# Attention kernel on one Trainium2 core: the values' low half, one context block and four rope products move between engines, and the roots move by a step

## The chip, the cores and the metric

The kernel runs on one core of a Trainium2 chip. The metric is the device time of one execution in microseconds (us), taken over several runs of the same program.

## The reference

A residual stream x of 4 sequences of 2048 rows by 256 channels goes through four layers, each of the form x = x + f(layernorm(x)): a layer that adds one row's projection to every row, a feed-forward layer, a banded attention layer and the feed-forward layer again. The attention layer is the one the change touches:

```python
q = _apply_rope(proj(Wq, bq)); k = _apply_rope(proj(Wk, bk)); v = proj(Wv, bv)
# 16 heads of 64, blocks of W = 128 rows; a block's queries see their own and the preceding block's keys, in a band
scores = jnp.einsum('bhnqd,bhnkd->bhnqk', qb, kcat) * scale
scores = jnp.where(valid[None, None], scores, -1e30)
attn = jax.nn.softmax(scores, axis=-1)
ctx = jnp.einsum('bhnqk,bhnkd->bhnqd', attn, vcat)
return merged @ Wo.T + bo
```

Rope multiplies each head's vector by cosines, and its swapped halves by sines. Every row block of a sequence has 256 keys, except the first of a sequence, which has 128.

## The kernel before, in words

The attention stage (attention_stage, from L867) works in 64 steps. A step t is one superblock S = t // 4 of four row blocks (512 rows) and one group g = t % 4 of four heads. Superblocks 0, 4, 8 and 12 begin a sequence: in their 16 steps block 0 is "alone", with 128 keys. Within a step the blocks b = 0..3 are numbered n = 4t + b.

Precision comes from splitting: a float32 value is written as a float16 high half and a float16 low half (value minus high half), and TensorE adds three products of halves. So the probabilities (prob) are split into halves, the contexts into c_halves, the values into v_h and v_l, the layer norm's rows into x_halves.

Each engine has its own fixed order, written out in a function at_step(t), and the engines meet only in semaphores. In one step:

- **TensorE** (L1739) projects queries, keys and values into two PSUM banks that these three share in turn (pr_ps, one bank per half), makes the scores of two blocks at a time (scores, L1709), multiplies turned probabilities by values (values_product, L1673, into the single bank c_ps), and makes a row block of the output (output, L1694). Values are made in values (L1623); then values_rest (L1641) adds minus the identity times v_h into the same bank, so that the bank holds value minus high half.
- **VectorE** (L1408) masks and scales the scores and takes their tops (tops, L1292, four instructions for a block), makes the probabilities' low half (p_low_of, L1308), scales the contexts (context, L1317: a reciprocal and a product), multiplies the second half of keys and queries by cosine and by sine straight from PSUM (key_product L1367, query_product L1377; two instructions each), and does the residual, layer norm moments and, once in four steps, shift_of.
- **ScalarE** (L1574) makes the exponentials, the probabilities' high half (p_high_of), v_h (v_high_of, L1477) and v_l (v_low_of, L1487), the contexts' high half (context_high), normalizes rows (normalize, x_high_of) and copies the first half of keys and queries out of PSUM (key_copy, query_copy).
- **GpSimd** (L1268) makes the rope products of the first halves from those copies (key_product, query_product), joins all products to keys and queries (key L1187, query L1198), makes the low halves of contexts (context_low) and rows (x_low_of), adds a bias (bias_rows), and once in four steps takes the roots of the layer norm (inverse_std, L1207). Twice in a step it waits for a low half of the probabilities of the same step before it goes on, and at its start for the last one of the step before (after_p_low, L1224).
- **SyncE** issues the transposing DMAs that turn probabilities, contexts and rows, and most loads.

GpSimd's order is the one that has to be followed in the prediction:

```python
after_p_low(t - 1, 3); x_low_of(t + 7)
if g == 0 and S > -2: inverse_std(S + 2)
context_low(t - 2); key_product(t + 1, 0); key_product(t + 1, 3)
after_p_low(t, 0); key(t + 1, 1); query_product(t + 1, 0)
after_p_low(t, 1); query_product(t + 1, 3); key(t + 1, 0)
query(t + 1, 1); query(t + 1, 0); bias_rows(t - 4)
```

x_low_of(t + 7) needs what ScalarE's normalize and x_high_of made a step earlier; scores(t + 1, 0) on TensorE needs both halves of keys and queries that end with query(t + 1, 0).

## Time and profile before

| what | value |
|---|---|
| median of 3 runs (range) | 1607.46 us (1604.61 to 1608.63) |
| the profiled execution's own time | 1604.13 us |
| its span, first to last instruction | 1602.3 us |
| mean granted TensorE clock | 0.985 |
| busy share of the span: TensorE, VectorE, ScalarE, GpSimd | 93%, 88%, 83%, 71% |
| a step in the middle of the attention stage | 17.9 to 19.7 us |

The profile page adds up each engine's busy time and lists the costliest groups of instructions. The trace also answers for a window of time: its timeline view prints every instruction with its start (us from the span's start) and its duration, and in brackets the idle time of the engine before it with what ended it. Neighbouring alike instructions are merged there, with their count at the end of the row. An instruction's duration includes a wait for a resource it finds taken. Starts of successive VectorE and ScalarE instructions lie some 0.08 to 0.10 us closer than their durations say, since they overlap.

### The profile page before, as it was taken

The page shows a single profiled execution, that of the slowest core. Times are in us where ns is not written, and L with a number is a line of the kernel's source. Part 1 is how long each engine was busy: PE and PEld are TensorE (multiplying, and loading weights), DVE is VectorE, ACT ScalarE, POOL GpSimd, SP SyncE. Part 2 cuts the span into 40 slices and gives each one's busy share as a digit, 9 for nine tenths or more (in the row PEclk, how much of TensorE's full clock was granted, in tenths as well). Part 3 has the DMA queues.
Part 4 walks back from the last instruction along what each step waited for, and adds up shares of the span by engine and source line. Part 5 has one row for each costly group of instructions (what it writes and reads, how often), then busy time and mean ns, then how long its engine had stood idle before and what let it go on. Part 6 is the DMA issues. An engine that isn't in the chain of part 4 may idle for free. (4 is left out here: it accounts for less than half of the span.)

```text
span 1602.3 us, 46976 instructions
## 1 busy us (share of the span) xinstructions
PE 1492.1 (93%) x16866; PEld 1142.8 (71%) x16866; DVE 1402.0 (88%) x3859; ACT 1324.3 (83%) x2442; POOL 1141.7 (71%) x911
## 2 busy tenths in 40 slices
PE   5999978899999999999999999999999999779998
PEld 4888745577777677766767777767776777668887
DVE  5999668999999999999999999999998999857885
ACT  5999768888888888888888888888888888749996
POOL 4665367778787887878787878787888777623443
PEclk8999989999999999999999999999999999979999
DMA  5232338899999999999999999999999998962331
GB/s 213 93 123 92 103 68 141 163 175 175 182 176 173 172 171 172 176 180 177 171 174 169 169 183 178 173 178 176 168 166 172 173 164 163 173 148 83 107 108 67
DMA packets 729886, 247.94 MB, mean 155 GB/s; under 512 B 689588, under 2 KB 716472, under 8 KB 729656
## 3 DMA queue, kind: packets, MB, share of 16 engines
q1 hardware_dynamic: 711816, 228.93, 75.8%
q10 hardware_dynamic: 17840, 16.00, 3.7%
q8 instruction: 137, 2.24, 0.6%
q14 instruction: 93, 0.76, 0.2%
HBM read 47.73 MB, written 25.17 MB: 45 GB/s over the span
## 5 line engine op out<-in xcount | busy, mean ns | idle before, releaser
L1302 DVE CUSTOM_DVE_ANT_0 at_prob<-banks,at_masks,pre_s_scale 128x256 f32<-128x256 f32 (+1 forms) x1024 | 421.2, 472 | 27.8 <-PE banks L1733 10.9
L1465 ACT ACTIVATE at_prob<-at_prob,at_top 128x256 f32<-128x256 f32 (+1 forms) x1024 | 428.3, 490 | 15.9 <-DVE at_top L1302 13.4
L1314 DVE TENSOR_TENSOR at_halves<-at_prob,at_halves 128x1024 f16<-128x1024 f32 (+1 forms) x256 | 330.7, 1292 | 3.1 <-ACT at_halves L1474 3.1
L1618 PE MATMUL banks<-at_xt,pre_w_h 128*128 128x512 f16 x1024 | 297.1, 382 | 12.1 <-ACT at_v_l L1493 9.1
L1733 PE MATMUL banks<-at_kt,at_qt 32*128 32x256 f32 (+1 forms) x4096 | 251.1, 381 | 40.9 <-POOL at_qt L1204 20.1
L1733 PEld LDWEIGHTS banks<-at_kt,at_qt 32*128 32x128 f32 x4096 | 197.0, 185 | 102.1 <-issue 97.6
L1474 ACT ACTIVATE at_halves<-at_prob 128x1024 f16<-128x1024 f32 (+1 forms) x256 | 263.3, 1029 | 6.1
L1194 POOL TENSOR_TENSOR at_kt<-at_k_by 128x512 f32<-128x512 f32 x128 | 173.8, 1358 | 65.4 <-DVE at_halves L1314 62.1
L1184 POOL TENSOR_TENSOR at_q_by<-at_q_first,at_tables 128x512 f32<-128x512 f32 x128 | 175.5, 1376 | 61.8 <-DVE at_halves L1314 59.6
L1689 PE MATMUL banks<-at_v_h,at_pt 128*128 128x65 f16 x1984 | 208.0, 195 | 10.1 <-DMA at_pt<-at_halves 7.0
L1689 PEld LDWEIGHTS banks<-at_v_h,at_pt 128*128 128x128 f16 x1984 | 182.0, 98 | 44.7 <-issue 23.0
L1204 POOL TENSOR_TENSOR at_qt<-at_q_by 128x512 f32<-128x512 f32 x128 | 212.2, 1678 | 0.0
L1690 PE MATMUL banks<-at_v_l,at_pt 128*128 128x64 f16 x1984 | 207.6, 193 | 0.0
L1691 PE MATMUL banks<-at_v_h,at_pt 128*128 128x65 f16 x1984 | 207.2, 194 | 0.0
L325 POOL TENSOR_TENSOR f_x<-f_x,f_gated 128x512 f32<-128x512 f32 x64 | 83.0, 1307 | 153.0 <-DVE f_gated L430 153.0
L1690 PEld LDWEIGHTS banks<-at_v_l,at_pt 128*128 128x128 f16 x1984 | 182.3, 99 | 8.7
L1691 PEld LDWEIGHTS banks<-at_v_h,at_pt 128*128 128x128 f16 x1984 | 182.6, 98 | 0.0
L1174 POOL TENSOR_TENSOR at_k_by<-at_k_first,at_tables 128x512 f32<-128x512 f32 x128 | 171.8, 1364 | 2.8 <-ACT at_k_first L1522 2.8
L1522 ACT ACTIVATE at_k_first<-banks,pre_bias 128x512 f32<-128x512 f32 x64 | 44.0, 687 | 154.4 <-PE banks L1618 154.4
L1618 PEld LDWEIGHTS banks<-at_xt,pre_w_h 128*128 128x128 f16 x1024 | 86.9, 98 | 113.8 <-issue 34.8
L1635 PE MATMUL banks<-pre_w_h,at_xt 128*128 128x256 f16 x1024 | 164.1, 273 | 0.9 <-ACT at_q_first L1532 0.8
L1618 PE MATMUL banks<-at_xt,pre_w_l 128*128 128x512 f16 x512 | 154.0, 383 | 0.0
(123 smaller groups left out, 3317.5 us busy)
## 6 DMA issues: line engine op xcount, KB each, us to landing
f_x<-in_x SPq DMA_DIRECT2D x16, 512.0 KB, 3.7
x_after_ffn<-f_x SPq DMA_DIRECT2D x16, 512.0 KB, 2.7
f_x<-x_after_attention SPq DMA_DIRECT2D x16, 512.0 KB, 4.3
out_x<-f_x SPq DMA_DIRECT2D x16, 512.0 KB, 3.0
at_x_res<-x_after_ffn ACTq DMA_DIRECT2D x61, 128.0 KB, 2.6
x_after_attention<-at_x_res ACTq DMA_DIRECT2D x58, 128.0 KB, 2.0
at_x_ln<-x_after_ffn SPq DMA_DIRECT2D x32, 128.0 KB, 3.0
at_tables<-in_cos SPq DMA_DIRECT2D x16, 256.0 KB, 3.5
```

What stands on the lines that cost most here:

```text
L1184: nc.gpsimd.tensor_tensor(q_by[:, n, :], q_first[:, :], tables[:, r, n // 3, :], ALU.mult).then_inc(q_made[n], 1)
L1194: nc.gpsimd.tensor_tensor(kt[:, half, own(t, 0):own(t, 0) + SB, :].rearrange("p s t -> p (s t)"), k_by[:, 2 * half, :], k_by[:, 2 * half + ...
L1204: nc.gpsimd.tensor_tensor(qt[:, t % 2, half, :], q_by[:, 2 * half, :], q_by[:, 2 * half + 1, :], (ALU.subtract, ALU.add)[half]).then_inc(q ...
L1302: last = nc.vector.tensor_tensor_reduce(out=prob[:, n % 2, h, low:2 * P], in0=s_ps[:, h, n % 2 * 2 * P + low:(n % 2 + 1) * 2 * P], in1=mas ...
L1314: nc.vector.tensor_tensor(parts[:, 1, :, :], prob[:, n % 2, :, keys_from(t, b):2 * P], parts[:, 0, :, :], ALU.subtract).then_inc(p_low, 1)
L1465: last = nc.scalar.activation(at, at, ACT.Exp, bias=top[:, n % 2, h:h + 1], scale=-1.0)
L1474: nc.scalar.activation(halves_of(n, alone(t, b))[:, 0, :, :], prob[:, n % 2, :, keys_from(t, b):2 * P], ACT.Copy).then_inc(p_high, 1)
L1618: last = nc.tensor.matmul(pr_ps[:, half, :].rearrange("p (b t) -> p b t", b=SB), w[wp][:, k, at:at + P], xt[:, r, :, xp, k, :], start=n == ...
L1689: nc.tensor.matmul(out, ph, v_h[:, at, h, :], start=s == 0, stop=False)
L1690: nc.tensor.matmul(out[:, 0:HD], ph, v_l[:, at, h, :], start=False, stop=False)
L1691: last = nc.tensor.matmul(out, pl, v_h[:, at, h, :], start=False, stop=s == len(slots) - 1)
L1733: last = nc.tensor.matmul(s_ps[:, h, d * 2 * P + keys_from(t, b):(d + 1) * 2 * P] .rearrange("p (s t) -> p s t", t=P), qt[rows_of, par, ha ...
```

## The change

- **Values.** TensorE's values_rest and the matrix neg_eye go, and ScalarE's two copies to v_l with them. VectorE makes v_l as the bank minus v_h (v_low_of, two instructions of 128x512 in a step), one before and one after the low half of block 2.
- **The first context of a step.** VectorE keeps the reciprocal (first_inverse). The product goes to ScalarE (first_context, four instructions of 128x64, one for each head, scaled by a pointer into inv), between the high half of block 3 and context_high.
- **Rope products of the second halves.** VectorE's two instructions of 128x512 become one of 128x1024 (key_products, query_products), with one semaphore in place of two; both query products now stand ahead of context(t - 1, 1). Semaphore names and the order of the slots in k_by and q_by follow.
- **Roots.** inverse_std goes from behind x_low_of in the steps with g = 0 to the end of the step before.

The diff, cut to its core (left out: declarations, the renamed semaphores of GpSimd's products, and query_products, which is written as key_products is):

```diff
--- before.py
+++ after.py
@@ -1270,20 +1264,20 @@
             after_p_low(t - 1, 3)
             if t + 7 >= SB:
                 x_low_of(t + 7)
-            if g == 0 and S > -2:
-                inverse_std(S + 2)
             context_low(t - 2)
             key_product(t + 1, 0)
-            key_product(t + 1, 3)
+            key_product(t + 1, 1)
             after_p_low(t, 0)
             key(t + 1, 1)
             query_product(t + 1, 0)
             after_p_low(t, 1)
-            query_product(t + 1, 3)
+            query_product(t + 1, 1)
             key(t + 1, 0)
             query(t + 1, 1)
             query(t + 1, 0)
             bias_rows(t - 4)
+            if g == 3 and S >= -2:
+                inverse_std(S + 3)
 
         return opening, first_std, set_ones, at_step
 
@@ -1330,6 +1324,24 @@
                                         src[:, :, 0:HD], inv[:, :, :].broadcast_to([P, GROUP, HD]),
                                         ALU.mult).then_inc(ctx_made, 1)
 
+        def first_inverse(t):
+
+            if step(t):
+                dve.wait_ge(pv_done, 4 * t + 1)
+                src = c_ps[:, 0:GROUP * VE].rearrange("p (h d) -> p h d", d=VE)
+                nc.vector.reciprocal(inv[:, :, :], src[:, :, HD:VE]).then_inc(inv_made, 1)
+
+        def v_low_of(t, half):
+
+            if step(t):
+                dve.wait_ge(v_high[half], t + 1)
+                if t < 2:
+                    dve.wait_ge(past.act_made, 2 * past.CHUNKS)
+                at = pair_of(t, half)
+                nc.vector.tensor_tensor(v_l[:, at, :, :],
+                                        pr_ps[:, half, :].rearrange("p (b h d) -> p b h d", b=2, d=HD),
+                                        v_h[:, at, :, 0:HD], ALU.subtract).then_inc(v_low[half], 1)
+
         def moments(n):
 
             if step(n):
@@ -1364,25 +1376,29 @@
                 nc.vector.scalar_tensor_tensor(x_res[:, i % RB, :], out_bank(i)[:, 0:C], pre.o_down[:, :],
                                                x_res[:, i % RB, :], ALU.mult, ALU.add).then_inc(x_made, 1)
 
-        def key_product(t, n):
+        def key_products(t):
 
             if step(t):
                 r, g = t // NG % 2, t % NG
                 dve.wait_ge(tab_in[r], tab_ready(t // NG))
                 dve.wait_ge(k_done[1], t + 1)
-                need(k_roped[n // 2], t)
-                nc.vector.scalar_tensor_tensor(k_by[:, n, :], pr_ps[:, 1, :], bias[:, 1, 2 * g + 1:2 * g + 2],
-                                               tables[:, r, n % 2, :], ALU.add, ALU.mult).then_inc(k_made[n], 1)
-
-        def query_product(t, n):
+                need(k_roped[0], t)
+                need(k_roped[1], t)
...
@@ -1409,23 +1425,23 @@
             S, g = divmod(t, NG)
             tops(t, 0)
             tops(t, 1)
-            query_product(t + 1, 2)
+            query_products(t + 1)
             context(t - 1, 1)
-            query_product(t + 1, 1)
             p_low_of(t, 0)
             tops(t, 2)
             context(t - 1, 2)
             p_low_of(t, 1)
             tops(t, 3)
             context(t - 1, 3)
+            v_low_of(t + 1, 1)
             p_low_of(t, 2)
+            v_low_of(t + 1, 0)
             residual(t - 5)
             if g == 0 and S > -2:
                 shift_of(S + 2)
             moments(t + 12)
-            context(t, 0)
-            key_product(t + 2, 1)
-            key_product(t + 2, 2)
+            first_inverse(t)
+            key_products(t + 2)
             p_low_of(t, 3)
 
         def last_step(next_moments, next_shift):
@@ -1440,7 +1456,7 @@
             tops(t, 3)
             context(t - 1, 3)
             p_low_of(t, 2)
-            context(t, 0)
+            first_inverse(t)
             p_low_of(t, 3)
             context(t, 1)
             residual(t - 5)
@@ -1484,15 +1500,18 @@
                                      pr_ps[:, half, :].rearrange("p (b h d) -> p b h d", b=2, d=HD),
                                      ACT.Copy).then_inc(v_high[half], 1)
 
-        def v_low_of(t, half):
-
-            if step(t):
-                act.wait_ge(v_rest[half], t + 1)
+        def first_context(t):
+
+            if step(t):
+                act.wait_ge(inv_made, 4 * t + 1)
+                need(ct_low, t - 1)
                 if t < 2:
-                    act.wait_ge(past.act_made, 2 * past.CHUNKS)
-                nc.scalar.activation(v_l[:, pair_of(t, half), :, :],
-                                     pr_ps[:, half, :].rearrange("p (b h d) -> p b h d", b=2, d=HD),
-                                     ACT.Copy).then_inc(v_low[half], 1)
+                    for c in (14, 15):
+                        act.wait_ge(past.moved[c % past.SLOTS], past.stores(c))
+                for h in range(GROUP):
+                    last = nc.scalar.activation(ctx[:, t % 2, 0, h * HD:(h + 1) * HD], c_ps[:, h * VE:h * VE + HD],
+                                                ACT.Copy, scale=inv[:, h, :])
+                last.then_inc(ctx_made, 1)
 
         def carry_keys(t):
 
@@ -1584,9 +1603,8 @@
             v_high_of(t + 1, 1)
             v_high_of(t + 1, 0)
             exponentials(t, 3)
-            v_low_of(t + 1, 1)
-            v_low_of(t + 1, 0)
             p_high_of(t, 3)
+            first_context(t)
             context_high(t - 1)
             store(t - 6)
             load_residual(t - 3)
@@ -1627,29 +1645,16 @@
                 if half == 0:
                     pe.wait_ge(q_copied, t + 1)
                 else:
-                    pe.wait_ge(q_made[1], t + 1)
-                    pe.wait_ge(q_made[2], t + 1)
+                    pe.wait_ge(q_second_made, t + 1)
                 for blk in range(2):
                     for n, (xp, wp) in enumerate(TERMS):
                         for k in range(CK):
                             last = nc.tensor.matmul(
                                 pr_ps[:, half, blk * 2 * P:(blk + 1) * 2 * P], xt[:, r, 2 * half + blk, xp, k, :],
                                 w[wp][:, k, VC + g * 2 * P:VC + (g + 1) * 2 * P],
-                                start=blk == 0 and n == 0 and k == 0, stop=False, skip_group_check=True)
+                                start=blk == 0 and n == 0 and k == 0, stop=blk == 1 and n == 2 and k == CK - 1,
+                                skip_group_check=True)
                 last.then_inc(v_done[half], 1)
-
-        def values_rest(t, half):
-
-            if step(t):
-                pe.wait_ge(v_high[half], t + 1)
-                if t == 0:
-                    pe.wait_ge(made, EYE_MADE)
-                for blk in range(2):
-                    last = nc.tensor.matmul(
-                        pr_ps[:, half, blk * 2 * P:(blk + 1) * 2 * P].rearrange("p (h d) -> p h d", d=HD),
-                        neg_eye[:, :], v_h[:, valued(t, 2 * half + blk), :, 0:HD], start=False, stop=blk == 1,
-                        skip_group_check=True)
-                last.then_inc(v_rest[half], 1)
 
         def keys_of(t, half):
 
@@ -1745,8 +1749,6 @@
             values(t + 1, 1)
             values_product(t - 1, 3)
             output(t - 5)
-            values_rest(t + 1, 1)
-            values_rest(t + 1, 0)
             values_product(t, 0)
             keys_of(t + 2, 1)
             scores(t + 1, 0)
```

In VectorE's queue, in the later half of a step, this stood before (at_halves is the low half of a block's probabilities, at_v_l the values' low half):

```order
L1323 RECIPROCAL at_inv<-banks 128x4
L1329 TENSOR_TENSOR at_ctx<-banks,at_inv 128x256
L1314 TENSOR_TENSOR at_halves<-at_prob,at_halves 128x1024
L1364 SCALAR_TENSOR_TENSOR at_x_res<-banks,pre_o_down,at_x_res 128x256
L1338 BN_STATS at_stats<-at_x_ln_odd 128x6
L1341 BN_AGGR at_mv<-at_stats 128x2
L1323 RECIPROCAL at_inv<-banks 128x4
L1329 TENSOR_TENSOR at_ctx<-banks,at_inv 128x256
L1374 SCALAR_TENSOR_TENSOR at_k_by<-banks,pre_bias,at_tables 128x512 x2
L1314 TENSOR_TENSOR at_halves<-at_prob,at_halves 128x1024
```

and this stands there in the changed kernel (in a step with g = 0, hence the at_shift row):

```order
L1317 RECIPROCAL at_inv<-banks 128x4
L1323 TENSOR_TENSOR at_ctx<-banks,at_inv 128x256
L1341 TENSOR_TENSOR at_v_l<-banks,at_v_h 128x2x256
L1308 TENSOR_TENSOR at_halves<-at_prob,at_halves 128x1024
L1341 TENSOR_TENSOR at_v_l<-banks,at_v_h 128x512
L1376 SCALAR_TENSOR_TENSOR at_x_res<-banks,pre_o_down,at_x_res 128x256
L1360 SCALAR_TENSOR_TENSOR at_shift<-at_mv,at_rstd 128x4
L1350 BN_STATS at_stats<-at_x_ln_odd 128x6
L1353 BN_AGGR at_mv<-at_stats 128x2
L1332 RECIPROCAL at_inv<-banks 128x4
L1387 SCALAR_TENSOR_TENSOR at_k_by<-banks,pre_bias,at_tables 128x1024
L1308 TENSOR_TENSOR at_halves<-at_prob,at_halves 128x1024
```

Two instructions have come in around block 2's low half, one product of the context has gone, and two key products have become one.

ScalarE's queue at the end of a step, in the changed kernel, with what each instruction waits for:

```order
L1490 ACTIVATE at_halves<-at_prob 128x1024 [waits at_pt_in1,at_p_made]
L1512 ACTIVATE at_ctx<-banks,at_inv 128x64 [waits at_ct_low,at_inv_made]
L1512 ACTIVATE at_ctx<-banks,at_inv 128x64 x3
L1532 ACTIVATE at_c_halves<-at_ctx 128x1024 [waits at_ct_in,at_ctx_made]
L1585 DMA x_after_attention<-at_x_res 128x256 [waits at_x_made]
L1579 DMA at_x_res<-x_after_ffn 128x256 [waits at_stored1]
L1559 ACTIVATE at_x_ln<-at_x_ln,at_shift,at_rstd 128x256 [waits at_shift_made]
L1571 ACTIVATE at_x_halves<-at_x_ln 128x256 [waits at_xt_in1,at_xn_made]
L1541 ACTIVATE at_k_first<-banks,pre_bias 128x512 [waits at_k_first_by_sin,at_k_first_by_cos,at_k_first_done]
```

The wait for at_inv_made, VectorE's reciprocal, is new here; before, two copies to at_v_l stood ahead of the at_halves row, and the four at_ctx instructions were not there.

## Rows read from the trace of the kernel before

**Rows 1.** The profile page: span, busy time of the engines, and two groups of TensorE.

```profile
span 1602.3 us, 46976 instructions
...
PE 1492.1 (93%) x16866; PEld 1142.8 (71%) x16866; DVE 1402.0 (88%) x3859; ACT 1324.3 (83%) x2442; POOL 1141.7 (71%) x911
...
L1618 PE MATMUL banks<-at_xt,pre_w_h 128*128 128x512 f16 x1024 | 297.1, 382 | 12.1 <-ACT at_v_l L1493 9.1
L1733 PE MATMUL banks<-at_kt,at_qt 32*128 32x256 f32 (+1 forms) x4096 | 251.1, 381 | 40.9 <-POOL at_qt L1204 20.1
```

**Rows 2.** Tile view of ScalarE's query copy: shortest, median, longest ns; first and last start.

```profile
L1532 ACT ACTIVATE at_q_first<-banks,pre_bias x64: 669/687/689, 208.8 to 1377.0; 128x512 f32<-128x512 f32 x64
```

**Rows 3.** ScalarE's timeline: five of these query copies, one in each step.

```profile
669.96 0.67 ACT L1532 ACTIVATE at_q_first<-banks,pre_bias 128x512 f32<-128x512 f32 x1
689.64 0.69 ACT L1532 ACTIVATE at_q_first<-banks,pre_bias 128x512 f32<-128x512 f32 x1
708.07 0.69 ACT L1532 ACTIVATE at_q_first<-banks,pre_bias 128x512 f32<-128x512 f32 x1
...
857.03 0.69 ACT L1532 ACTIVATE at_q_first<-banks,pre_bias 128x512 f32<-128x512 f32 x1 [0.81 <-PE banks L1618]
874.99 0.69 ACT L1532 ACTIVATE at_q_first<-banks,pre_bias 128x512 f32<-128x512 f32 x1 [0.80 <-PE banks L1618]
```

**Rows 4.** GpSimd's timeline, 690 to 709.8 us.

```profile
696.49 1.27 POOL L1194 TENSOR_TENSOR at_kt<-at_k_by 128x512 f32<-128x512 f32 x1
697.72 3.48 POOL L1204 TENSOR_TENSOR at_qt<-at_q_by 128x512 f32<-128x512 f32 x2
...
703.58 0.67 POOL L1221 TENSOR_TENSOR at_x_halves<-at_x_ln,at_x_halves 128x256 f16<-128x256 f32 x1 [1.69 <-DVE at_halves L1314]
...
706.32 2.50 POOL L1174 TENSOR_TENSOR at_k_by<-at_k_first,at_tables 128x512 f32<-128x512 f32 x2
```

**Rows 5.** VectorE's timeline over the same stretch.

```profile
693.82 1.35 DVE L1314 TENSOR_TENSOR at_halves<-at_prob,at_halves 128x1024 f16<-128x1024 f32 x1
...
697.49 1.35 DVE L1314 TENSOR_TENSOR at_halves<-at_prob,at_halves 128x1024 f16<-128x1024 f32 x1
...
699.70 0.15 DVE L1323 RECIPROCAL at_inv<-banks 128x4 f32<-128x4 f32 x1
699.89 0.43 DVE L1329 TENSOR_TENSOR at_ctx<-banks,at_inv 128x256 f32<-128x256 f32 x1
700.96 1.41 DVE L1374 SCALAR_TENSOR_TENSOR at_k_by<-banks,pre_bias,at_tables 128x512 f32<-128x512 f32 x2 [0.65 <-PE banks L1618]
702.29 1.21 DVE L1314 TENSOR_TENSOR at_halves<-at_prob,at_halves 128x1024 f16<-128x1024 f32 x1
...
706.83 0.75 DVE L1384 SCALAR_TENSOR_TENSOR at_q_by<-banks,pre_bias,at_tables 128x512 f32<-128x512 f32 x1
...
708.71 1.22 DVE L1314 TENSOR_TENSOR at_halves<-at_prob,at_halves 128x1024 f16<-128x1024 f32 x1
```

**Rows 6.** ScalarE's timeline over the same stretch.

```profile
699.62 1.05 ACT L1474 ACTIVATE at_halves<-at_prob 128x1024 f16<-128x1024 f32 x1
700.57 1.05 ACT L1513 ACTIVATE at_c_halves<-at_ctx 128x1024 f16<-128x1024 f32 x1
...
702.14 0.42 ACT L1552 ACTIVATE at_x_halves<-at_x_ln 128x256 f16<-128x256 f32 x1
```

**Rows 7.** GpSimd's timeline in a step with g = 0: the roots.

```profile
666.59 1.02 POOL L1214 TENSOR_TENSOR at_rstd<-at_veps,at_power 128x4 f32<-128x4 f32 x1
```

**Rows 8.** TensorE's timeline, 828.6 to 829.2 us: the product with minus the identity.

```profile
828.66 0.61 PE L1648 MATMUL banks<-at_v_h,at_neg_eye 128*128 128x256 f16 x4
```

**Rows 9.** Groups of instructions kept apart by shape, whole span: busy us, mean ns.

```profile
L430 DVE TENSOR_TENSOR f_gated<-banks,f_gate 128x512 f32<-128x512 f32 x64 | 42.5, 682 | 12.4 <-PE banks L703 7.3 <-ACT f_gate L565 3.1 <-issue 2.0
...
L1465 ACT ACTIVATE at_prob<-at_prob,at_top 128x256 f32<-128x256 f32 x960 | 408.1, 497 | 15.9 <-DVE at_top L1302 13.4
L1465 ACT ACTIVATE at_prob<-at_prob,at_top 128x128 f32<-128x128 f32 x64 | 20.2, 389 | 0.0
```

66 lines of the change are left out of this document (33 added, 33 removed).

## The prediction, made before the changed kernel ran

> **What bounds the kernel now.** I read the page first. TensorE is busy for 93% of the span and VectorE for 88% [rows 1], and TensorE's two telling waits are 9.1 us for ScalarE's copy to v_l and 20.1 us for GpSimd's queries. That looks like a kernel bound by TensorE, for which the change takes work away. But the busy time of pipelined products says little, so I read steps next. ScalarE's query copy comes once in a step, 64 times from 208.8 to 1377.0 us [rows 2]: 63 steps of 18.54 us on average, 73% of the span. A plain step takes 708.07 - 689.64 = 18.43 us, a step after roots 19.68, an "alone" step (128 keys in block 0) 874.99 - 857.03 = 17.96 [rows 3].
>
> Then I laid the timelines of a plain step side by side and asked what releases what. I set 0 at the end of block 1's low half, 693.82 + 1.35 = 695.17 us [rows 5]. Two things show.
>
> First, a low half on VectorE and an instruction of GpSimd exclude each other. GpSimd's keys end at 696.49 + 1.27 = 697.76 [rows 4]; block 2's low half, asked for at 697.49, ends at 698.84, 1.08 us after them, and takes 1.35 us where an undisturbed one takes 1.21 [rows 5]. GpSimd's two query instructions behind it take 3.48 us together [rows 4], 1 us more than two of 1.27 (minus 0.04 of overlap): the first stood until the low half ended. VectorE's query products (PSUM and one tile in SBUF) ran beside the last GpSimd product of 706.32 + 2.50 [rows 4, 5], and neither grew.
>
> Second, the period is the round of four legs from low half to low half, by their ends: block 1 to block 2, 698.84 - 695.17 = 3.67 us; block 2 to block 3 (702.29 + 1.21 = 703.50), 4.66; block 3 to block 0 (708.71 + 1.22 = 709.93), 6.43; block 0 to block 1 again, the rest of 18.43, 3.67 [rows 3, 5]. The third leg is GpSimd's: it starts its row halves at 703.58, right behind block 3's low half, works without a pause until 708.82, and VectorE's block 0, asked for at 708.71, ends 1.11 us later [rows 4, 5]. VectorE idles 0.65 us in the second leg, for TensorE. So VectorE and GpSimd are tied together with under a microsecond of slack.
>
> **The change, part by part.**
>
> *TensorE.* Four products go, 0.44 us a step (0.61 for the four with the tail of the last [rows 8]), and a wait for v_l, 9.1 us in all [rows 1]. All this lies beside the round above. TensorE loses work that nobody waits for any longer: worth 0, and 28 us (64 times 0.44) if the round were TensorE's.
>
> *VectorE.* Added: two subtractions of 128x512 with one input in PSUM. The nearest row, the gate's product of the same shape, has 0.682 us [rows 9], less 0.08 of overlap: 0.60 each (bounds: 0.55 and 0.67, the latter a rope product's distance of start to start, half of 702.29 - 700.96 [rows 5]). Merging two products saves one fixed part: 0.67 + 0.67 becomes 0.67 + 512 elements at about 1.04 ns (between 0.43 us for 256 and 0.682 for 512 [rows 5, 9] one element costs 1.0), so 1.20 instead of 1.33, twice a step, -0.27 with rounding. The first context's product leaves with its own wait, 0.42. Net: 1.20 - 0.27 - 0.42 = +0.5 us of VectorE a step, less than its idle 0.65. Counted like this the change would be free. What matters is where the first subtraction stands.
>
> *Leg 1.* Block 2's low half was asked for at 2.32. It now comes behind a subtraction, at 2.92. But GpSimd's keys end at 2.59 and the first query instruction runs from 2.55 to 3.82 [rows 4]. The low half is held for that whole instruction and ends at 3.82 + 1.08 = 4.90 in place of 3.67: 0.60 of work and 0.63 of waiting. GpSimd is where it was, since its second query instruction is held instead of the first: both end at 6.03, and the scores start as before.
>
> *Leg 2.* From the low half's end to the reciprocal it was 699.70 - 698.84 = 0.86 [rows 5]; with the second subtraction 1.46, so at 6.36. Key products at 6.46 (no wait: TensorE delivers keys earlier now), low half of block 3 at 7.66 to 8.87. The leg is 3.97 in place of 4.66.
>
> *ScalarE.* It loses two copies and gains a wait. first_context needs that reciprocal, done at 6.53; ScalarE has finished block 3's high half long before (old end 700.67, and two copies less ahead of it). Behind the waiting instruction stand context_high, the stores, the normalization and x_high, and GpSimd's row halves need the last. Four instructions of 128x64 with a pointer: exponentials, which also have one, take 497 ns for 256 and 389 for 128 [rows 9], so 335 for 64, and 0.24 from start to start: 3 x 0.24 + 0.34 - 0.10 = 0.96. Plain copies are shorter (0.42 for 256 [rows 6]), 0.26 for 64, which gives 0.64. I take 0.90, nearer the pointer's row. From context_high's start to x_high's end it is 702.56 - 700.57 = 1.99 [rows 6]. So x_high ends at 6.59 + 0.90 + 1.99 = 9.48; it used to end at 7.39, a microsecond before GpSimd asked.
> The Trainium skill, ScalarE: Activation LUTs, section What ACT_TABLE_LOAD costs, gives 280 ns plus 0.833 ns an element for an instruction with a pointer and 93 ns of overlap; for these four that is 0.96, and my sum would be some 3 us more by it.
>
> *Leg 3.* GpSimd starts its row halves at 9.53, not at 8.95 behind block 3's low half, and ends the key products 5.24 later (703.58 to 708.82 [rows 4]), at 14.77. From block 3's low half to the query products VectorE has the tops of two blocks, 706.83 - 703.50 = 3.33 [rows 5], of which I count 0.16 as a wait for TensorE that will be over. Then come the merged product and the context (0.55), so it gets to block 0 at 8.87 + 3.17 + 1.20 + 0.55 = 13.79, finds GpSimd's last product begun at 13.50, and ends at 14.77 + 1.08 = 15.85. The leg is 6.98 in place of 6.43.
>
> *Leg 4* is untouched, 3.67. Sum: 4.90 + 3.97 + 6.98 + 3.67 = **19.52**, +1.09 us in a plain step.
>
> *Roots.* They cost a step 19.68 - 18.43 = 1.25 us, and the step before it is 0.15 to 0.2 shorter: 1.05 for each of 14. In the new place they wait for the normalization (done at 9.05), and take 0.28 + 1.0 [rows 7]: row halves start at 10.4 instead of 9.53. Then VectorE comes to block 0 before GpSimd's last product has begun and goes first; that step is 19.0, the next pays with 20.1, and the pair is as long as two plain ones. So the 1.05 is saved.
>
> *Alone steps.* Four tops of 128 are 0.54 us shorter, so VectorE comes to block 0 at 13.25, while GpSimd's last product but one runs (to 13.5). The short low half ends at 14.1, GpSimd's last product at 15.2, its keys and query product at 17.7, and block 1's low half 1.08 later: 18.8 in place of 17.96.
>
> **The sum.** Ten superblocks are plain with roots: 4 x 1.09 - 1.05 = +3.3 each, 33 us. Four are alone: 4 x 0.85 less 1.05, with rounding +2.5, 10 us. The last two have no roots: +4.4, 9 us. The first and last steps, in which the queues fill and drain and the slack is larger, I take off with 4. Together +48, on the profiled execution's own 1604.1 (span 1602.3): **1652 us**. The median of the runs shown is 3.3 us above that execution; I leave this in the range. With the bounds of the subtraction and of the four instructions the sum runs from +27 to +60: 1631 to 1664 is this case's own range.
>
> **The rivals.**
> - *Only the first hold (1626 us, chance 0.14).* If the four context instructions take 0.5 us or less, or ScalarE gets past them early, row halves start near 8.95 and a step is 18.95: about +22 us.
> - *The round stays loose, faster (1581 us, 0.14).* If block 2's low half slips in ahead of GpSimd's first query instruction, which is decided at 2.55 (a subtraction of 0.25 us would do, or GpSimd giving way), no hold is added. The round then runs through the merged query products, 0.13 us shorter: 63 x 0.13 = 8, and 14 roots at 1.05 = 15, together -23. For it: TensorE has work taken away and its waits on v_l end. Against: the rows show no 512 elements in 0.25 us, and block 2's low half waited for GpSimd even by 0.14.
> - *The subtractions are held too (1720 us, 0.05).* They read an SBUF tile, as a low half does. Asked for at 2.32 and 4.8, each would meet an instruction of GpSimd, 0.3 and 0.8 us: 1.1 a step, 63 x 1.1 = 69 us on top of 1652. Against: the query products, of the same kind of operands, ran freely.
> The Trainium skill, SBUF — State Buffer, section SBUF: two separate sides, says that a VectorE instruction with two SBUF inputs and a GpSimd instruction lock each other out for a whole instruction. By that rule the low halves are held and the subtractions are not; the rows here agree for the low halves (1.08 us after GpSimd's end), and no row shows a subtraction.
> - *No change (1604 us, 0.07).* Holds and the saved roots cancel: a plain step of some 18.7.
>
> **How the numbers follow.** The likeliest case has 0.60. Measured differences under 0.3%, 5 us, count as no change here. Faster 0.14, same 0.07, slower 0.79. The range of 1595 to 1672 takes in the first and last rivals and leaves out most of the fast one and the slowest, 0.2 together.
>
> **What would show it.** Right: a plain step of 19.3 to 19.7 us; block 2's low halves of 1.9 to 2.0 us where they were 1.35; ScalarE idle some 1.9 us before first_context with VectorE's reciprocal as the releaser; GpSimd's row halves released by ScalarE's x_high and no longer by a low half; TensorE busy below 90%; roots steps in pairs of 19.0 and 20.1. Wrong: subtractions beyond 0.75 us (held), low halves of block 2 near 1.2 us (no hold), a plain step under 18.4, or row halves still released by block 3's low half.

## The result, and the profile after

The changed kernel takes 1649.61 us (median of 4 runs, 1648.24 to 1650.34), against 1608.05 (1604.61 to 1609.73, 4 runs) for the kernel before: a ratio of 1.026, 95% interval 1.0247 to 1.0274. It is slower by some 42 us. The forecast was 1652, in a range of 1595 to 1672.

The profile page, with the lines that answer to [rows 1]:

```profile
span 1646.2 us, 46365 instructions
...
PE 1484.5 (90%) x16610; PEld 1124.4 (68%) x16610; DVE 1477.1 (90%) x3795; ACT 1329.3 (81%) x2570; POOL 1139.7 (69%) x909
...
L1308 DVE TENSOR_TENSOR at_halves<-at_prob,at_halves 128x1024 f16<-128x1024 f32 (+1 forms) x256 | 389.1, 1520 | 3.2 <-ACT at_halves L1490 3.2
...
L1636 PE MATMUL banks<-at_xt,pre_w_h 128*128 128x512 f16 x1024 | 301.2, 387 | 7.8 <-DVE at_v_l L1341 4.4
```

TensorE is down from 93% to 90% of the span, VectorE up from 88 to 90. The low halves alone cost VectorE 389.1 us, where the profile page of before has 330.7; the instruction that did not grow in work (1.21 us undisturbed, [rows 5]) now has a mean of 1520 ns, so at least 0.31 us of each of 256 is waiting on average (0.08 before). TensorE's wait for v_l fell from 9.1 to 4.4 us, and bought nothing.

The list of waits (us in total, times, longest) names three that the kernel before did not have at this size; the at_ctx one is wholly new, and GpSimd's row halves were released by a low half in [rows 4]:

```profile
ACT at_ctx L1512 <- DVE at_inv L1332: 107.8, 63, 2.0
POOL at_x_halves L1220 <- ACT at_x_halves L1571: 100.5, 43, 3.1
...
PE banks L1737 <- POOL at_qt L1203: 27.9, 13, 2.5
```

A plain step, from query copy to query copy, is 746.97 - 727.49 = 19.48 us. VectorE's timeline in it, to be read against [rows 5]:

```profile
728.03 2.06 DVE L1308 TENSOR_TENSOR at_halves<-at_prob,at_halves 128x1024 f16<-128x1024 f32 x1
...
732.41 1.35 DVE L1308 TENSOR_TENSOR at_halves<-at_prob,at_halves 128x1024 f16<-128x1024 f32 x1
...
736.08 0.68 DVE L1341 TENSOR_TENSOR at_v_l<-banks,at_v_h 128x512 f16<-128x512 f32 x1
736.68 1.98 DVE L1308 TENSOR_TENSOR at_halves<-at_prob,at_halves 128x1024 f16<-128x1024 f32 x1
738.58 0.68 DVE L1341 TENSOR_TENSOR at_v_l<-banks,at_v_h 128x512 f16<-128x512 f32 x1
...
740.12 0.15 DVE L1332 RECIPROCAL at_inv<-banks 128x4 f32<-128x4 f32 x1
...
741.40 1.22 DVE L1308 TENSOR_TENSOR at_halves<-at_prob,at_halves 128x1024 f16<-128x1024 f32 x1
...
747.52 2.05 DVE L1308 TENSOR_TENSOR at_halves<-at_prob,at_halves 128x1024 f16<-128x1024 f32 x1
```

ScalarE's, against [rows 6]:

```profile
737.38 1.06 ACT L1490 ACTIVATE at_halves<-at_prob 128x1024 f16<-128x1024 f32 x1
740.30 0.52 ACT L1512 ACTIVATE at_ctx<-banks,at_inv 128x64 f32<-128x64 f32 x2 [1.86 <-DVE at_inv L1332]
...
740.71 0.52 ACT L1512 ACTIVATE at_ctx<-banks,at_inv 128x64 f32<-128x64 f32 x2
...
741.10 1.07 ACT L1532 ACTIVATE at_c_halves<-at_ctx 128x1024 f16<-128x1024 f32 x1
...
742.70 0.42 ACT L1571 ACTIVATE at_x_halves<-at_x_ln 128x256 f16<-128x256 f32 x1
```

GpSimd's, against [rows 4]:

```profile
736.31 3.48 POOL L1203 TENSOR_TENSOR at_qt<-at_q_by 128x512 f32<-128x512 f32 x2
...
743.25 0.67 POOL L1220 TENSOR_TENSOR at_x_halves<-at_x_ln,at_x_halves 128x256 f16<-128x256 f32 x1 [2.79 <-ACT at_x_halves L1571]
```

The reader sees the chain in three places. VectorE's first subtraction pushes block 2's low half behind the start of GpSimd's first query instruction, and it takes 1.98 us instead of 1.35. The second subtraction and that delay carry the reciprocal to 740.12. ScalarE stands idle for 1.86 us waiting for it, with the row normalization queued behind, and GpSimd stands idle for 2.79 us waiting for the rows.

### The profile page after: what moved, and what is told of

It is laid out like the page before. It is cut to its first block and busy times, and to the rows that moved or that the text cites. A ratio compares the mean times of both kernels' runs of the same rounds, so it can differ in the third digit from the quotient of the medians.

```text
span 1646.2 us, 46365 instructions
## 1 busy us (share of the span) xinstructions
PE 1484.5 (90%) x16610; PEld 1124.4 (68%) x16610; DVE 1477.1 (90%) x3795; ACT 1329.3 (81%) x2570; POOL 1139.7 (69%) x909
## 5 line engine op out<-in xcount | busy, mean ns | idle before, releaser
L1308 DVE TENSOR_TENSOR at_halves<-at_prob,at_halves 128x1024 f16<-128x1024 f32 (+1 forms) x256 | 389.1, 1520 | 3.2 <-ACT at_halves L1490 3.2
L1737 PE MATMUL banks<-at_kt,at_qt 32*128 32x256 f32 (+1 forms) x4096 | 260.1, 391 | 86.2 <-issue 55.6
L1636 PE MATMUL banks<-at_xt,pre_w_h 128*128 128x512 f16 x1024 | 301.2, 387 | 7.8 <-DVE at_v_l L1341 4.4
L1737 PEld LDWEIGHTS banks<-at_kt,at_qt 32*128 32x128 f32 x4096 | 203.5, 190 | 147.8 <-issue 143.2
L1203 POOL TENSOR_TENSOR at_qt<-at_q_by 128x512 f32<-128x512 f32 x128 | 221.9, 1756 | 0.0
L1193 POOL TENSOR_TENSOR at_kt<-at_k_by 128x512 f32<-128x512 f32 x128 | 163.3, 1275 | 58.0 <-DVE at_halves L1308 55.3
L1173 POOL TENSOR_TENSOR at_k_by<-at_k_first,at_tables 128x512 f32<-128x512 f32 x128 | 175.1, 1390 | 10.1 <-ACT at_k_first L1541 10.1
L1232 POOL TENSOR_TENSOR at_c_halves<-at_ctx,at_c_halves 128x1024 f16<-128x1024 f32 x64 | 136.8, 2137 | 15.8 <-DVE at_halves L1308 10.6
```

What stands on the lines that cost most here:

```text
L1173: nc.gpsimd.tensor_tensor(k_by[:, n, :], k_first[:, :], tables[:, r, n, :], ALU.mult).then_inc(k_first_made[n], 1)
L1203: nc.gpsimd.tensor_tensor(qt[:, t % 2, half, :], q_by[:, half, :], q_by[:, 3 - half, :], (ALU.subtract, ALU.add)[half]).then_inc(q_roped[h ...
L1308: nc.vector.tensor_tensor(parts[:, 1, :, :], prob[:, n % 2, :, keys_from(t, b):2 * P], parts[:, 0, :, :], ALU.subtract).then_inc(p_low, 1)
L1636: last = nc.tensor.matmul(pr_ps[:, half, :].rearrange("p (b t) -> p b t", b=SB), w[wp][:, k, at:at + P], xt[:, r, :, xp, k, :], start=n == ...
L1737: last = nc.tensor.matmul(s_ps[:, h, d * 2 * P + keys_from(t, b):(d + 1) * 2 * P] .rearrange("p (s t) -> p s t", t=P), qt[rows_of, par, ha ...
```

## The experiments

Two theories were left to tell apart after the result. By the first, **two orders** cost the time: the first subtraction ahead of a low half, and the first context ahead of the normalization. By its rivals it is the **work itself**, moved to the busiest engine, or to ScalarE. The roots and TensorE's part were open as well. Below, every ratio is to the kernel before (median 1605.61, 1606.18 and 1605.99 us in the three batches of runs), and a plain step is the distance of query copies as in [rows 3]. Runs of different batches are compared by their ratios, of which 0.001 is 1.6 us.

**The roots alone.** The kernel before, with only this:

```diff
-            if g == 0 and S > -2:
-                inverse_std(S + 2)
...
+            if g == 3 and S >= -2:
+                inverse_std(S + 3)
```

> The kernel before with the roots moved alone. My theory: the roots' instructions fall into GpSimd's wait for block 3's low half, every one of the 14 groups of four steps is 1.05 us shorter, so about 15 us less than before, near 1593 us, and the steps of 19.6 us are gone. Rival (the roots only shift the wait, to the normalization or to the next step): within 3 us of before, with steps of 19.6 us left.

Measured: 1603.37 us, ratio 0.9986 (0.9976 to 0.9997). The move gives 2 us, not 15. GpSimd's timeline in such a step says why:

```profile
664.44 0.20 POOL L1212 TENSOR_TENSOR at_veps<-at_mv,at_eps 128x4 f32<-128x4 f32 x1 [0.71 <-ACT at_x_ln_odd L1540]
664.72 1.97 POOL L1214 TENSOR_TENSOR at_rstd<-at_veps,at_power 128x4 f32<-128x4 f32 x1
666.67 0.67 POOL L1221 TENSOR_TENSOR at_x_halves<-at_x_ln_odd,at_x_halves 128x256 f16<-128x256 f32 x1
```

The roots may not overwrite rstd before ScalarE has normalized, so they start at 664.44. VectorE's low half of block 3 runs from 664.61 to 665.82 there, and the root instruction, 1.02 us long in [rows 7], now takes 1.97. It ends 0.85 us after the time at which GpSimd would have started its row halves. In ten of the 14 steps with roots it is the instruction ahead of it, at_veps, that is caught: it takes 1.29 us in place of 0.20, at_rstd runs its 1.02 behind the low half, and the row halves start about 1.1 us late. So the roots' time comes behind the low half in their new place too; the step behind them is 19.2 to 19.5 us long in the plain superblocks, where it was 19.5 to 19.8. The theory behind the 15 us fell.

**Both subtractions behind the low half.** The changed kernel, with v_low_of(t + 1, 1) one place later:

```diff
-            v_low_of(t + 1, 1)
             p_low_of(t, 2)
+            v_low_of(t + 1, 1)
             v_low_of(t + 1, 0)
```

> The changed kernel with both subtractions for the values behind block 2's low half. My theory: the hold of 0.6 us on that low half goes (1.35 us again instead of 1.98), ScalarE still waits for the reciprocal, and its x_high is what GpSimd waits for: a plain step of about 18.8 us, and the whole near that of before, 1600 to 1612 us. Rival (VectorE's added work is what costs, wherever it stands): as the changed kernel, 1645 to 1650 us.

Measured: 1617.38 us, ratio 1.0074 (1.0055 to 1.0092), plain step 18.85. The step is as expected and the low halves of block 2 in it take 1.35 us again; the whole is 5 us above the expected range.

**The first context behind the normalization.** The changed kernel, with first_context moved on ScalarE:

```diff
             p_high_of(t, 3)
-            first_context(t)
             context_high(t - 1)
...
+            first_context(t)
             key_copy(t + 2)
```

> The changed kernel with ScalarE's first context behind the normalization and x_high of the step. My theory: only the hold on block 2's low half is left of the two causes: a plain step of 18.95 us, about 1620 to 1628 us. Rival (ScalarE's wait is harmless, the hold makes all of the loss): as the changed kernel, 1645 to 1650 us. Second rival (the wait makes all of it): under 1600 us.

Measured: 1616.53 us, ratio 1.007 (1.005 to 1.0091), plain step 18.92, as expected; the whole is 3.5 us under the expected range. The low half of block 2 is held as before the mend:

```profile
744.02 1.98 DVE L1308 TENSOR_TENSOR at_halves<-at_prob,at_halves 128x1024 f16<-128x1024 f32 x1
```

**Both mended.**

> The changed kernel with both edits: both subtractions behind block 2's low half, the first context behind x_high. My theory: the round of VectorE and GpSimd is as tight as before, a plain step of 18.3 us and no stall for the roots: 1585 to 1592 us, under both kernels, 5 or so below the roots alone. Rival (VectorE's or TensorE's work is the bound and not the order): over 1600 us.

Measured: 1599.85 us, ratio 0.9966 (0.9953 to 0.998), plain step 18.45. In a last batch the same kernel ran again:

> The kernel of x4_both once more, beside the other three on the same chip: 0.9953 to 0.998 of the kernel before, 1598 to 1602 us, if the gain is real; over 0.999 if it was one batch's.

Measured: 1602.33 us, ratio 0.9967 (0.9954 to 0.998). All the work that the change moves is still moved, and the kernel is faster than both, by 0.3%. So the two orders made the loss of 42 us, not the work. By the ratios, 1.026 against 1.0074, 1.007 and 0.9966, each mend alone takes off some 30 us (0.019 of 1606) and both together 47. Were the delays apart, it would be 60: they lie one behind the other in the same round, and with one gone, a part of the other is taken up by slack. The expectation of 1585 to 1592 was too good, for it counted on a step of 18.3 and on roots that cost nothing.

**A late low half without more work.** The kernel before, with the residual ahead of block 2's low half instead of behind it, which delays that low half and adds no work:

```diff
-            p_low_of(t, 2)
             residual(t - 5)
+            p_low_of(t, 2)
```

> The kernel before with one order changed: VectorE's residual, 0.39 us that it does anyway, stands ahead of block 2's low half and no longer behind it. No work is added. Theory of the hold: the low half is asked for at 2.71 us after block 1's, when GpSimd's first query instruction has begun (2.55 to 3.82), so it takes about 2.2 us in place of 1.35; VectorE's idle 0.65 us ahead of the key products takes most of that up, and the kernel is 0 to 10 us slower. Rival (low halves are lengthened by something else, such as memory traffic in general): they stay at 1.35 us and the time is unchanged.

Measured: 1611.15 us, ratio 1.0028 (1.0017 to 1.004), plain step 18.42. VectorE's timeline in a step whose query copy starts at 690.86:

```profile
699.59 0.48 DVE L1364 SCALAR_TENSOR_TENSOR at_x_res<-banks,pre_o_down,at_x_res 128x256 f32<-128x256 f32 x1 [0.81 <-PE banks L1705]
699.99 1.29 DVE L1314 TENSOR_TENSOR at_halves<-at_prob,at_halves 128x1024 f16<-128x1024 f32 x1
...
703.60 1.21 DVE L1314 TENSOR_TENSOR at_halves<-at_prob,at_halves 128x1024 f16<-128x1024 f32 x1
```

Counted from its query copy, block 2's low half ends at 10.42 us, against 698.84 - 689.64 = 9.20 in the kernel before [rows 3, 5]: 1.2 us late. Block 3's ends at 13.95, against 13.86. VectorE's idle time in front of the key products, 0.65 us in [rows 5], is gone, and the residual's 0.39 behind the low half too. The delay did not come about as expected, though: here the residual waits 0.81 us for TensorE's output, and the low half, asked for when the first query instruction is nearly over, takes 1.29 us and not 2.2. The expected hold is there in three other steps, where the residual does not wait, as in the one that starts at 786.14:

```profile
794.68 2.07 DVE L1314 TENSOR_TENSOR at_halves<-at_prob,at_halves 128x1024 f16<-128x1024 f32 x1
```

By the ends of the low halves the leg from block 1 to block 2 is 4.90 us in these three steps, exactly that of the changed kernel, and the next leg is 3.53. The two together are 8.43, against 3.67 + 4.66 = 8.33 in the kernel before. So a late or held low half costs 0.1 us at most while that slack pays for it. In the changed kernel, with the second subtraction in the next leg, that leg is 3.96 and not 3.53, and the slack no longer pays. The whole kernel is still 4.5 us slower than before, by a few steps in which the residual waits and the low half is held as well (a leg of 5.9 to 6.1 us).

**TensorE's part alone.** The kernel before without the product with minus the identity. It leaves out the subtraction, so that the low half of the values is wrong; it serves for the time only:

```diff
-            values_rest(t + 1, 1)
-            values_rest(t + 1, 0)
...
-                act.wait_ge(v_rest[half], t + 1)
+                act.wait_ge(v_done[half], t + 1)
```

> The kernel before without TensorE's product with minus the identity and nothing else changed: the low half of the values is then a copy of the whole value, which leaves out the subtraction. My theory: TensorE is not the bound, its 0.44 us a step are worth at most a few us: 1600 to 1606 us, plain steps stay at 18.4. Rival (the round is TensorE's): 28 us less, near 1578 us, a plain step of 18.0.

Measured: 1608.34 us, ratio 1.0011 (1 to 1.0021), plain step 18.42, with this on the page:

```profile
PE 1473.7 (92%) x16610; PEld 1123.9 (70%) x16610; DVE 1403.0 (87%) x3859; ACT 1323.8 (82%) x2442; POOL 1137.6 (71%) x911
...
L1618 PE MATMUL banks<-at_xt,pre_w_h 128*128 128x512 f16 x1024 | 297.7, 383 | 31.0 <-ACT at_v_l L1493 27.4
```

TensorE lost 18.4 us of busy time, and its wait for v_l grew from 9.1 to 27.4 us: what was taken from it came back as waiting. An engine at 93% was not the bound.

**The first context alone.** The kernel before, with only first_inverse and first_context, in the places of the change.

> The kernel before with only the first context's product moved to ScalarE, ahead of context_high. My theory: without the hold the reciprocal is there before ScalarE's high half ends, there is no wait, x_high ends at about 8.2 us where GpSimd asks for it at 8.4, so the time stays within 5 us of before. Rival (the 0.8 us of ScalarE's work lie on the path): 30 to 50 us slower.

Measured: 1606.33 us, ratio 0.9998 (0.9988 to 1.0008). With the low half of block 2 on time the reciprocal is early, and ScalarE waits for it in two of the 64 steps only, 0.72 and 0.99 us; this is one of them:

```profile
720.45 0.31 ACT L1513 ACTIVATE at_ctx<-banks,at_inv 128x64 f32<-128x64 f32 x1 [0.72 <-DVE at_inv L1338]
```

**More room on VectorE.** Both orders mended, and the residual ahead of block 0's low half, moments and shift behind the key products, to make the reciprocal early and the middle legs short.

> As x4_both, with VectorE's work shifted out of the leg between block 2's and block 3's low half: the residual goes ahead of block 0's low half, where VectorE waits for GpSimd anyway (0.4 us), and shift_of behind the key products, where GpSimd is idle and doesn't hold it (0.8 us in the steps with g = 0 become 0.1). My theory: a plain step of 18.05 to 18.2 us, no longer step with g = 0, 1572 to 1582 us in all. Rival (another round, through TensorE or ScalarE, lies just below): within 5 us of x4_both, near 1600 us.

Measured: 1638 us, ratio 1.0193 (1.0175 to 1.0212), plain step 19.09. This theory fell as well. VectorE's timeline shows the reciprocal early, as wanted, and then a hole:

```profile
716.05 1.28 DVE L1341 TENSOR_TENSOR at_v_l<-banks,at_v_h 128x512 f16<-128x512 f32 x2
717.25 0.17 DVE L1332 RECIPROCAL at_inv<-banks 128x4 f32<-128x4 f32 x1
718.42 1.28 DVE L1387 SCALAR_TENSOR_TENSOR at_k_by<-banks,pre_bias,at_tables 128x1024 f32<-128x1024 f32 x1 [1.01 <-issue]
```

TensorE's timeline names what the key products wait for. Its keys go into the bank that the first subtraction reads:

```profile
716.87 0.59 PE L1637 MATMUL banks<-at_xt,pre_w_h 128*128 128x512 f16 x2 [0.98 <-DVE at_v_l L1341]
```

The way is subtraction, TensorE's keys, VectorE's key products. Residual and moments had been standing in that time, and once they are moved away VectorE waits instead, with the same work left to do elsewhere. By the ends of the low halves the leg from block 2 to block 3 is 5.24 us here and 4.71 with both orders mended, which is 0.53 of the 0.64 that the step is longer.

**The shift alone moved.** Both orders mended, and only in the steps with g = 0 shift_of and moments behind the key products.

> Both orders mended (as in x4_both), and in the steps with g = 0 VectorE's shift_of and moments stand behind the key products. Theory: in those steps the shift (0.83 us, held by GpSimd's query instruction) delays the reciprocal and with it the contexts, x_high and GpSimd's row halves; behind the key products it delays only block 3's low half, so a step with g = 0 goes from 18.9 to 18.6-18.7 us, and the whole kernel is 3 to 5 us faster than x4_both: some 1595 us. Rival, from x8_loose: moments had covered TensorE's keys, the key products wait for them, and the step stays at 18.9 or longer: 1600 us or more.

Measured: 1603.78 us, ratio 0.998 (0.997 to 0.999). The rival held. The shift takes 0.15 us there, where it took 0.86 beside GpSimd's query instruction, and VectorE waits 0.62 us for its keys in front of the key products:

```profile
680.46 1.28 DVE L1387 SCALAR_TENSOR_TENSOR at_k_by<-banks,pre_bias,at_tables 128x1024 f32<-128x1024 f32 x1 [0.62 <-issue]
681.66 0.15 DVE L1360 SCALAR_TENSOR_TENSOR at_shift<-at_mv,at_rstd 128x4 f32<-128x4 f32 x1
```

The step is 18.91 us long, against 18.94 with the shift in its old place.

**The roots, undone, in two kernels.** First in the one with both orders mended:

> Both orders mended, inverse_std back behind x_low_of in the steps with g = 0. Theory: once ScalarE normalizes early, the roots' new place lies in GpSimd's wait for the last low half and costs little, while the old place costs the step 1.0 us; with 14 of them and the step behind taking part of it back, this is 5 to 12 us slower than x4_both: 1605 to 1612 us. Rival: the roots' place is worth nothing in this kernel either (as in x1_roots, where the move gave 2 us): within 3 us of x4_both.

Measured: 1607.94 us, ratio 1.0011 (0.9999 to 1.0022), and 1602.33 for its partner with the roots moved: the move is worth 5.6 us here (7 by the ratios). In the partner ScalarE normalizes early, and the roots lie wholly in front of GpSimd's wait for block 3's low half, as its timeline in the same step of the first run of that kernel shows:

```profile
662.13 1.02 POOL L1213 TENSOR_TENSOR at_rstd<-at_veps,at_power 128x4 f32<-128x4 f32 x1
663.64 0.67 POOL L1220 TENSOR_TENSOR at_x_halves<-at_x_ln_odd,at_x_halves 128x256 f16<-128x256 f32 x1 [0.49 <-DVE at_halves L1308]
```

Then in the changed kernel:

> The changed kernel with inverse_std back in its old place and nothing else undone. By the prediction's term the moved roots save 1.05 us in each of 14 steps here, so this would be 15 us slower: 1664 us. By the theory from x1_roots (the roots wait for ScalarE's normalization wherever they stand, and are held by a low half there) the move is worth 2 to 5 us: 1652 to 1655 us. Third: in the changed kernel GpSimd waits for x_high anyway, so that in the old place they add all of their length: 14 us again.

Measured: 1655.57 us, ratio 1.031 (1.0295 to 1.0325): the move is worth 6 us there by the medians, which are of different batches, and 8 by the ratios. Where the clock of TensorE stays up (below), the two steps of a superblock that differ are 20.16 + 18.73 us long in this kernel, and 19.71 + 18.74 in the changed one: 0.44 us saved, 14 times, is 6. So one edit of the change, with the same code, is worth 2, 6 and 6 us in three kernels, and 15 in none.

## Why the prediction was right, and where it was not

**The round: right.** The step was forecast at 19.52 us and is 19.48. By the ends of the low halves the legs are 738.66 - 733.76 = 4.90 (forecast 4.90), 742.62 - 738.66 = 3.96 (3.97), 19.48 less the other three = 6.95 (6.98), and 733.76 - 730.09 = 3.67 (3.67). The subtraction takes 0.68 us and 0.60 from start to start, as the gate's row [rows 9] had it, and is not held. The reciprocal was placed 6.36 us after the end of block 1's low half and is there at 740.12 - 733.76 = 6.36; x_high was to end at 9.48 and ends at 9.36. The rule of the Trainium skill, SBUF — State Buffer, section SBUF: two separate sides, that the prediction took for its rival, agrees with these rows: the low halves, with two inputs in SBUF, are held, and the subtraction, with one in PSUM, is not.

**The four context instructions: a size.** Forecast 0.90 us, measured 741.10 - 740.30 = 0.80. One takes 315 ns, and they start 0.205 us apart, not 0.24: neighbours overlap by 0.11 us here. By the figures of the Trainium skill, ScalarE: Activation LUTs, section What ACT_TABLE_LOAD costs, one would take 333 ns and the four 0.96, as an estimate; the measurement lies half-way between that and the lower bound of the sum, 0.64.

**The last two superblocks: the step that failed.** The sum gave them +4.4 us each, as if their steps were plain. The two together are 1.0 us longer than before, where 8.8 was forecast. What is absent there has no term in the sum. Rows of a late step that still normalizes, and of one that does not:

```profile
1298.95 1.98 DVE L1308 TENSOR_TENSOR at_halves<-at_prob,at_halves 128x1024 f16<-128x1024 f32 x1
...
1305.00 0.67 POOL L1220 TENSOR_TENSOR at_x_halves<-at_x_ln_odd,at_x_halves 128x256 f16<-128x256 f32 x1 [2.25 <-ACT at_x_halves L1571]
...
1373.30 1.98 DVE L1308 TENSOR_TENSOR at_halves<-at_prob,at_halves 128x1024 f16<-128x1024 f32 x1
...
1378.75 2.13 POOL L1232 TENSOR_TENSOR at_c_halves<-at_ctx,at_c_halves 128x1024 f16<-128x1024 f32 x1 [1.65 <-DVE at_halves L1308]
```

The first delay acts to the end: block 2's low half takes 1.98 us and its leg is 4.90. But from the superblock before on VectorE has no moments left to take (they run twelve steps ahead), and the second leg is 3.38 us, where it was 3.96. The kernel before gains nothing by that: its second leg stays 4.64, and VectorE waits 1.06 us for TensorE in it. While rows are still normalized the second delay acts too, with a third leg of 7.0, and three steps in a row, the first of them in the superblock before, are 18.95 to 18.98 us. Once none are left, GpSimd has no x_high to wait for and is released by block 3's low half; the third leg is 6.33, and the steps are 18.3 us (one is 18.74), under the 18.42 of the kernel before. That 18.95 is also the number of the rival "only the first hold" is chance, for both delays act in those three steps.

**The roots: mis-sized.** 15 us were taken off for them. The runs show 6 in the changed kernel and 2 alone. Alone, the prediction's error was to take the roots' 1.0 us as whole once they start; it did not ask what VectorE would be doing then. In the changed kernel the error was the price in the old place, 1.05 us. With the roots there, four steps of a superblock are 20.16 + 18.73 + 2 x 19.48 = 77.85 us long, and four plain ones 77.92: they cost nothing any more. With the roots moved they are 77.41 long, less than four plain ones. The low halves of VectorE's timeline show how a disturbed round can be shorter. First block 0's in the plain step that holds the roots, then blocks 0, 1 and 2 of the step behind, then block 0's of the next:

```profile
670.11 2.06 DVE L1308 TENSOR_TENSOR at_halves<-at_prob,at_halves 128x1024 f16<-128x1024 f32 x1
...
689.58 1.65 DVE L1308 TENSOR_TENSOR at_halves<-at_prob,at_halves 128x1024 f16<-128x1024 f32 x1
693.56 1.30 DVE L1308 TENSOR_TENSOR at_halves<-at_prob,at_halves 128x1024 f16<-128x1024 f32 x1
697.77 1.76 DVE L1308 TENSOR_TENSOR at_halves<-at_prob,at_halves 128x1024 f16<-128x1024 f32 x1
...
709.26 1.35 DVE L1308 TENSOR_TENSOR at_halves<-at_prob,at_halves 128x1024 f16<-128x1024 f32 x1
```

A plain step holds this low half for 0.85 us (2.06 less 1.21), since it meets GpSimd's last product just begun. Behind the roots GpSimd is late, the two meet elsewhere, and less is lost: 0.44, and 0.14 in the next step. Counted as the prediction did, from block 1's low half to block 1's, the pair was to be 19.0 and 20.1. It is 694.86 - 675.83 = 19.03, and then 19.42: the first is right, and the second does not pay back. A superblock was to be 3.3 us longer than before; the four of this kind behind the first in which TensorE's clock stays up are 1.7 to 2.6 us longer.

**TensorE's clock: not in the sum.** In five steps of 21.35 us the granted clock falls. The step of the changed kernel that starts at 610.1 is one of them. TensorE's timeline:

```profile
620.07 0.59 PE L1636 MATMUL banks<-at_xt,pre_w_h 128*128 128x512 f16 x2
623.06 2.96 PE L1737 MATMUL banks<-at_kt,at_qt 32*128 32x256 f32 x32 [2.39 <-POOL at_qt L1203]
```

and the busy time of the engines by stretches (PE, PEld, DVE, ACT, POOL, then PEclk, DMA share, GB/s):

```profile
618.00:621.00 3.00, 2.67 (x35) 1.43 (x32) 3.00 (x4) 2.60 (x5) 3.00 (x3) 1.00 0.91 175
621.00:623.00 2.00, 0.00 (x0) 0.00 (x0) 1.97 (x7) 0.59 (x3) 2.00 (x3) 1.00 0.63 122
623.00:626.00 3.00, 2.94 (x33) 2.32 (x34) 1.73 (x2) 2.19 (x5) 1.29 (x3) 0.66 1.13 230
626.00:628.00 2.00, 2.00 (x10) 0.77 (x9) 1.94 (x9) 0.00 (x0) 2.00 (x2) 0.65 0.26 65
628.00:632.00 4.00, 4.00 (x49) 2.38 (x51) 3.13 (x12) 3.82 (x7) 2.64 (x3) 1.00 0.52 101
```

TensorE is idle from 620.67 to 623.06, since GpSimd's queries are late. Then for 5 us the granted clock is 0.65 on average, between its levels of 2.4 and 1.2 GHz, and the 32 score products take 2.96 us, where the same 32 take 2.01 elsewhere. 5 x 0.35 = 1.7 us is lost, and the step is 21.36 - 19.71 = 1.65 longer than its likes. Five of them make 8 us, all of it in plain superblocks. In two more steps, of 20.29 and 20.48 us, the clock fell as well; the second is in a superblock of "alone" steps that is 2 us longer than the other three. In other such steps the clock stayed at 1.00, after a short wait for the same queries and after one as long:

```profile
701.98 2.01 PE L1737 MATMUL banks<-at_kt,at_qt 32*128 32x256 f32 x32 [1.24 <-POOL at_qt L1203]
...
779.43 2.01 PE L1737 MATMUL banks<-at_kt,at_qt 32*128 32x256 f32 x32 [2.41 <-POOL at_qt L1203]
```

So the length of this wait does not decide it alone. Ahead of six of the falls this wait is 1.85 to 2.41 us, and in two "alone" superblocks the clock stayed at 1.00 after 2.53 and 2.54. What decides stays open.

In the kernel with the roots undone there are nine long steps, of 21.3 to 21.8 us, each with a granted clock of 0.92 on average, and in one of them the score products took 3.30 us behind a wait of 2.40. That would be the gap between the 6 us worked out for the roots and the 10 us by which the 63 steps of that profiled run are longer.

**The sum.** The 63 steps together are 40.4 us longer than before, the first query copy comes 2.5 us later and the tail is 1 longer: 43.9, the difference of the spans. The 2.5 may be no work of the change: in its two profiled executions the kernel with both orders mended has that copy at 209.45 and at 211.26. The 4 us that the prediction took off for the first and last steps cannot be told apart in the runs. By superblocks, ten plain ones give +29.4 (forecast 33), the four at the beginning of a sequence +10.0 (10), the last two +1.0 (8.8). Some 10 us of the clock lie in the first two of these numbers. Without them the whole would be 34 us, where 48 were forecast: so a part of the good agreement is luck, the clock's loss standing in for terms that were too large (8 us in the last superblocks, the rest in the steps behind the roots). The mechanism, and the length of the plain step, are no luck.

**The rivals.** That TensorE's removed work would be worth 28 us fell with the run that removes it alone. "The subtractions are held too" fell with their 0.68 us. "Only the first hold" was right in its step, worked out as 18.95: the changed kernel with ScalarE's order mended has 18.92. Its sum was too large, for that kernel is 11 us slower than before (1.007) and not 22. "The round stays loose" fell as a forecast, and its condition was half of what is needed: with block 2's low half ahead of the first query instruction alone the plain step is 18.85 us, and with ScalarE's order mended as well 18.45, not the 18.30 that was worked out. That kernel is 4 to 6 us faster than before and not 23. Of the 15 us for the roots in that number 6 were there, and the plain step did not get shorter by the merged query products. What sets 18.45 us was not taken apart further. Of the signs that the prediction named, two were missed narrowly or in part: TensorE's busy share is 90.2% and not below 90, and the pairs behind the roots were not 19.0 and 20.1.

## What to carry over

- When work is handed to an engine that takes turns with another one for SBUF, look at the instruction that comes next in its queue, and at what the other engine starts in the time that is added. Here 0.6 us of new work put a low half behind one instruction start, and this and one wait queued ahead of a normalization turned a gain of 0.3% into a loss of 2.6%. Both were mended by moving one line each.
- A step that is moved is worth what the queue around it makes of it: the same move gave 2 us or 6. And idle-looking fillers can be covers: the residual and moments stood in the time in which TensorE made keys, and moving them away cost some 37 us (a ratio of 1.0193 against 0.9966).
- Before multiplying a price by the number of steps, count the steps in which work is absent (here no moments and no rows left to normalize) and take their legs apart as well.

## What was not expected of the hardware

- The exclusion of VectorE and GpSimd holds for tiny instructions too. A 128x4 instruction of GpSimd (at_rstd, 1.02 us) took 1.97 us when it met a low half in the kernel with only the roots moved, at_veps (0.20 us) took 1.29 there in ten steps, and a 128x4 instruction of VectorE (at_shift) took 0.86 us where 0.15 was seen elsewhere. In the kernel with both orders mended it stood beside GpSimd's second query instruction, which ended at 679.66 as it did. In these rows what such an instruction costs is set by the one it meets, not by its own length.

```profile
678.82 0.86 DVE L1360 SCALAR_TENSOR_TENSOR at_shift<-at_mv,at_rstd 128x4 f32<-128x4 f32 x1
```

- TensorE's granted clock fell after 2.39 us of idle time in a stretch that was busy otherwise, and in a like step of the same execution stayed at 1.00 after 2.41 us. Where it fell, the same lateness of the queries cost 1.65 us more.
- Four ScalarE instructions of 128x64 with a pointer as scale follow each other at 0.205 us, although each is reported as 0.315 us long.
